# A two-layer transformer block on one core: attention's value products by four heads, row maxima over two banks, and first maxima made a row ahead

## The reference, cut to what matters

```
qkv = x @ w_qkv + b_qkv                      # (8, 512, 384), 16 heads of 8 channels
att = einsum('bhqd,bhkd->bhqk', q, k) / sqrt(8)
att = where(causal, att, -inf)
y   = einsum('bhqk,bhkd->bhqd', softmax(att), v)
x1  = x + gate * (y @ w_proj + b_proj)
```

## Time and profile before

| what | value |
|---|---|
| runs shown, median (lowest to highest) | 3398.66 us (3397.5 to 3406.68) |
| span of the profiled execution | 3389.5 us |
| outside the span, against the median | 9.2 us |
| PE busy / DVE / ACT / POOL | 76% / 55% / 47% / 28% |
| mean granted clock of TensorE | 0.834 |
| DMA, mean | 29 GB/s |

### The profile page before, as it was taken

The page is one execution under the profiler, slowest core; times in us unless marked ns, Lnnn a source line. Parts: engine busy times, 40 slices in busy tenths (PEclk is TensorE's granted clock), DMA queues, the critical chain, the costliest instruction groups (busy, mean ns, idle before and its releaser), DMA issues. The chain is left out here.

```text
span 3389.5 us, 65593 instructions
## 1 busy us (share of the span) xinstructions
PE 2579.8 (76%) x23476; PEld 1819.6 (54%) x23508; DVE 1865.9 (55%) x4776; ACT 1591.1 (47%) x3545; POOL 932.4 (28%) x641
## 2 busy tenths in 40 slices
PE   2486888778788787878879678786888868787787
PEld 1254764456644565446645367453664447644565
DVE  2337654576445664466643765537655476545664
ACT  0137453474435643365434754338443474435644
POOL 1105330143303432043220442105330143302332
PEclk8588887888878888788878888789887888878888
DMA  3300011010110101001020010200002000110101
GB/s 96 84 5 10 14 26 73 4 15 12 38 60 1 16 15 59 35 3 16 13 89 5 5 18 9 89 5 10 13 19 80 4 13 13 33 64 4 16 15 42
DMA packets 213726, 96.60 MB, mean 29 GB/s; under 512 B 175978, under 2 KB 204530, under 8 KB 209754
## 3 DMA queue, kind: packets, MB, share of 16 engines
q1 hardware_dynamic: 209160, 90.02, 10.0%
q10 hardware_dynamic: 4224, 2.10, 0.2%
HBM read 70.88 MB, written 21.17 MB: 27 GB/s over the span
## 5 line engine op out<-in xcount | busy, mean ns | idle before, releaser
L1695 POOL TENSOR_TENSOR arena<-upto,gk 128x1536 f32<-128x1536 f32 x32 | 88.1, 2754 | 941.2 <-DVE beta L1142 941.2
L1149 DVE SCALAR_TENSOR_TENSOR arena<-bank,conv,arena 128x510 f32<-128x510 f32 (+1 forms) x384 | 285.7, 748 | 71.4 <-ACT arena L1442 47.8
L1687 POOL TENSOR_TENSOR arena<-arena 128x511 f32<-128x511 f32 x192 | 243.9, 1270 | 205.1 <-DVE arena L1149 204.9
L1036 DVE TENSOR_REDUCE mx<-bank 128x1 f32<-128x128 f32 (+3 forms) x512 | 219.0, 486 | 136.2 <-PE bank L515 131.2
L678 PE MATMUL bank<-h_t,arena 128*128 128x512 f32 x384 | 228.3, 690 | 57.1 <-DVE arena L1149 57.0
L514 PE MATMUL bank<-vq 72*128 72x128 bf16 (+3 forms) x512 | 180.9, 414 | 98.3 <-DMA vq<-qk_bounce 49.7
L1405 ACT ACTIVATE arena<-bank 128x384 f32<-128x384 f32 (+1 forms) x384 | 174.1, 538 | 166.2 <-PE bank L542 166.2
L1527 ACT COPY u<-bank 32x192 f32<-32x192 f32 x128 | 39.9, 312 | 400.2 <-PE bank L812 398.7
L1739 POOL TENSOR_TENSOR arena<-arena 128x1536 f32<-128x1536 f32 x24 | 82.5, 3437 | 422.7 <-DVE arena L1278 227.3
L469 PE MATMUL bank<-ident,xn 128*128 128x128 f32 x132 | 36.8, 435 | 169.5 <-DVE xn L987 169.5
L735 PE MATMUL bank<-vq 64*128 64x128 f32 x1536 | 117.2, 305 | 57.5 <-ACT arena L1516 36.5
(11 more groups left out here) (290 smaller groups left out, 6435.6 us busy)
## 6 DMA issues: line engine op xcount, KB each, us to landing
arena<-w_bounce SPq DMA_DIRECT2D x16, 1024.0 KB, 8.5
vq<-qk_bounce SPq DMA_DIRECT2D x27, 384.0 KB
vq<-qk_bounce SPq DMA_DIRECT2D x9, 1152.0 KB
qk_bounce<-qkp SPq DMA_DIRECT2D x54, 128.0 KB, 2.3
arena<-in_L_attn_Wv_dram SPq DMA_DIRECT2D x8, 768.0 KB, 11.7
t<-t_bounce SPq DMA_DIRECT2D x256, 12.0 KB, 1.8
x<-t_bounce SPq DMA_DIRECT2D x256, 12.0 KB, 1.8
arena<-in_L_attn_Wq_dram SPq DMA_DIRECT2D x8, 384.0 KB, 8.7
```

The lines of the kernel that those rows point to most:

```text
L1036: last = V.reduce_max(mx[:, h, t:t + 1], score_bank(n)[:, 0:(t + 1) * P], AX.X)
L1149: ins = V.scalar_tensor_tensor(a[:, k:T], ps[:, 0:T - k], conv[:, n, 3 - k:4 - k], a[:, k:T], ALU.mult, ALU.add)
L1687: G.tensor_tensor(acc[:, n % 4, 1:T], acc[:, n % 4, 1:T], acc2[:, n % 3, 0:T - 1], ALU.add).then_inc(taps_added, 1)
```

## The change

It does these things.

- The maxima are made in 22 units of one instruction each: a unit is one query tile t of 8, 4, 2 or 2 heads, spread over two neighbouring banks (1024 or 768 columns), with one mask matmul per bank. All eight banks become one PSUM tensor, so that one reduction can span two.
- Heads are grouped by eight for the maxima: two groups, two trips through DRAM (`maxima(b, i)` on SP) in place of four.
- The first group of the next row (units 0 to 10, `scores(b, 1, u)` on PE and `row_max(b, 1, u)` on DVE) is made at the end of the row: units 0 and 1 between the transposes and the projection of `project(3)`, 2 and 3 before the last norm, 4 to 6 after the second, third and fourth feed-forward matmul, 7 to 10 after the second product; on DVE 7 to 10 and the splitting stand behind L1343. For the first row this is done ahead of the loop.
- The feed-forward matmuls use two banks in place of four and wait for the gelu of two before.
- Value products take four heads at once, with `p_t` in two buffers of four heads; each four heads are transposed (`turn`) and divided as soon as they are copied.
- `scores_t` has one mask matmul for the bank with two key tiles.
- The transfers into the stacks are twelve without broadcast, of 8 rows (nine for q) and 24 rows (three for k), in place of four; `stacks_in` goes from 80 to 208.
- POOL fills v's constant columns behind the splitting of q and k. SP serves the first maxima of a row before the loads of weights.

The diff, cut to its core (counts, bank tables and the parts that only follow are left out):

```diff
+        HALF = [(t, range(h, h + n)) for t, n in enumerate((8, 4, 2, 2)) for h in range(0, HG, n)]
+        NU = len(HALF)
+        UNITS = [(t, range(hs.start + HG * i, hs.stop + HG * i)) for i in range(2) for t, hs in HALF]
...
         def score_t_bank(h, i):
-            return PS[3 + i if h < 10 or h % 2 else i]
+            return PS[(3, 4, 6)[i] if h >= HG and h % 2 == 0 else i]
...
         def f_bank(j):
-            return PS[2 + j]
-
-        f2_bank = PS[6]
+            return PS[6 + j % 2]
+
+        f2_bank = PS[5]
...
             if c + 1 == NT:
-                stages += [("enter_qkv", 1), ("enter_q", 1), ("enter_k", 1)]
+                stages += [("enter_q", 1), ("enter_k", 1), ("enter_qkv", 1)]
...
+            def scores(b, ahead, u):
+
+                t, hs = UNITS[u]
+                if u == 0:
+                    pe.wait_ge(stacks_in, at(b, stacks_in, IN_ROW["stacks_in"], ahead))
+                    pe.wait_ge(v_ready, at(b, v_ready, 1, ahead))
+                elif u == NU:
+                    pe.wait_ge(s_max, at(b, s_max, NU - 1, ahead))
+                elif u != 1 and u != NU + 1:
+                    pe.wait_ge(s_max, at(b, s_max, u - 1, ahead))
+                e = (t + 1) * P
+                per_bank = len(hs) // 2
+                for i in range(2):
+                    ps = PS[unit_banks(u)[0] + i][:, 0:per_bank * e].rearrange("p (h w) -> p h w", h=per_bank)
+                    for j in range(per_bank):
+                        h = hs[per_bank * i + j]
+                        mm(ps[:, j, :], q_stack[0:KS, h, t * P:e], k_stack[0:KS, h, 0:e], start=(j == 0), stop=False)
+                    last = mm(ps[:, :, t * P:e], ident_bf[:, :], mask_q[:, 0:per_bank, :], start=False, stop=True)
+                last.then_inc(s_ps, 1)
...
+                def weigh(g):
+
+                    if g:
+                        pe.wait_ge(y_sb, at(b, y_sb, g))
+                    else:
+                        pe.wait_ge(v_pads, at(b, v_pads, 1))
+                        pe.wait_ge(x_done, at(b, x_done, 1))
+                    pe.wait_ge(p_ready, at(b, p_ready, 12 * g + 12))
                     c0 = 0
                     for j in range(NT):
                         n = T - j * P
-                        for h in (2 * pair, 2 * pair + 1):
-                            r = 32 * (h % 4)
-                            last = mm(y_bank[r:r + 32, j * P:T], v32[:, j, h, :], p_t[:, h % 4, c0:c0 + n],
+                        for i in range(4):
+                            last = mm(y_bank[32 * i:32 * i + 32, j * P:T], v32[:, j, 4 * g + i, :], p_t[g % 2][:, i, c0:c0 + n],
...
+                scores(b, 0, NU)
+                scores(b, 0, NU + 1)
+                move_maxima(0)
+                for u in range(NU + 2, NU + 6):
+                    scores(b, 0, u)
+                scores_t(0)
+                scores(b, 0, NU + 6)
+                scores_t(1)
+                scores(b, 0, NU + 7)
+                scores_t(2)
+                scores(b, 0, NU + 8)
+                scores(b, 0, NU + 9)
+                scores_t(3)
+                scores(b, 0, NU + 10)
+                scores_t(4)
+                weigh(0)
+                move_maxima(1)
+                for h in range(5, 9):
                     scores_t(h)
+                weigh(1)
+                scores_t(9)
+                turn(0)
+                for h in range(10, 13):
+                    scores_t(h)
+                weigh(2)
+                turn(1)
+                for h in range(13, HA):
+                    scores_t(h)
+                turn(2)
+                weigh(3)
+                turn(3)
...
+                    if c + 1 == NT:
+                        scores(b, 1, 0)
+                        scores(b, 1, 1)
+                    ps = wo_bank(c)
...
+                scores(b, 1, 2)
+                scores(b, 1, 3)
                 layer_norm(LEAVE)
...
                 for j in range(FT):
+                    if j >= 2:
+                        pe.wait_ge(f_sb, at(b, f_sb, j - 1))
                     mm(f_bank(j)[:, :], w1[:, j * P:(j + 1) * P], h_t[:, :], start=True, stop=True).then_inc(f_ps, 1)
+                    if j:
+                        scores(b, 1, 3 + j)
...
                 last.then_inc(f2_ps, 1)
-                pe.wait_ge(rt_d, at(b, rt_d, 1))
+                for u in range(7, NU):
+                    scores(b, 1, u)
...
+            def row_max(b, ahead, u):
+
+                t, hs = UNITS[u]
+                dve.wait_ge(s_ps, at(b, s_ps, u + 1, ahead))
+                dst = mx[:, hs.start:hs.stop, t].rearrange("p (i h) -> p i h", i=2)
+                V.reduce_max(dst, unit_scores(u), AX.X).then_inc(s_max, 1)
...
                 V.tensor_tensor(xs[:, :, :], xs[:, :, :], xn[:, :, :], ALU.add).then_inc(x_done, 1)
+                for u in range(7, NU):
+                    row_max(b, 1, u)
+                split_maxima(b, 1, 0)
...
                 for part in range(PARTS):
-                    of_part = qk_bounce[0, part].rearrange("d h t -> d (h t)").unsqueeze(0).to_broadcast([PARTS, DA, HA * T])
-                    sp.dma_start(q_stack[PARTS * DA * part:PARTS * DA * (part + 1), :, :].rearrange("p h t -> p (h t)"), of_part).then_inc(stacks_in, 16)
+                    of_part = qk_bounce[0, part].rearrange("d h t -> d (h t)")
+                    for r in range(PARTS * DA * part, PARTS * DA * (part + 1), DA):
+                        sp.dma_start(q_stack[r:r + DA, :, :].rearrange("p h t -> p (h t)"), of_part).then_inc(stacks_in, 16)
                 sp.wait_ge(parts_out[1], at(b, parts_out[1], 16 * PARTS, ahead))
-                all_parts = qk_bounce[1].rearrange("n d h t -> (n d) (h t)").unsqueeze(0).to_broadcast([PARTS, PARTS * DA, HA * T])
-                sp.dma_start(k_stack[0:KS, :, :].rearrange("p h t -> p (h t)"), all_parts).then_inc(stacks_in, 16)
+                all_parts = qk_bounce[1].rearrange("n d h t -> (n d) (h t)")
+                for r in range(0, KS, PARTS * DA):
+                    sp.dma_start(k_stack[r:r + PARTS * DA, :, :].rearrange("p h t -> p (h t)"), all_parts).then_inc(stacks_in, 16)
```

More of the change, by code:

```diff
@@ L85, in dram @@
             return nc.dram_tensor(name, shape, dt).ap()
-        PS = [ctx.enter_context(nc.psum_tensor(f"bank{i}", [P, 512], F32)) for i in range(8)]
+        banks = ctx.enter_context(nc.psum_tensor("bank", [P, 8 * 512], F32))
+        PS = [banks[:, 512 * i:512 * (i + 1)] for i in range(8)]
         def sig(name):
@@ L483, in enter_qkv @@
                 last.then_inc(v_ps, 1)
+            def scores(b, ahead, u):
[8 more added lines that the diff above has]
+                e = (t + 1) * P
+                per_bank = len(hs) // 2
+                for i in range(2):
[5 more added lines that the diff above has]
+                last.then_inc(s_ps, 1)
             enter_norm(0, 0)
             enter_qkv(0, 0)
+            for u in range(NU):
+                scores(0, 0, u)
             with pe.Fori(0, NB) as b:
@@ L559, in weigh @@
                     last.then_inc(pv_ps, 1)
-                LAG = 8
-                for h in range(LAG):
-                    scores(h)
-                    if h == 5:
-                        move_maxima(0)
-                for h in range(HA):
-                    if h + LAG < HA:
-                        scores(h + LAG)
-                    scores_t(h)
-                    if h in (1, 5, 9):
-                        move_maxima(h // 4 + 1)
-                    if h % 2 and h > 1:
-                        weigh(h // 2 - 1)
@@ L1028, in tiles @@
                     return ps[:, :].rearrange("p (c d) -> p c d", c=NT)
+                for u in range(NU, 2 * NU):
+                    row_max(b, 0, u)
+                split_maxima(b, 0, 1)
                 for g in range(4):
-                    for h in range(HG * g, HG * g + HG):
-                        for t in range(NT):
-                            n = h * NT + t
-                            dve.wait_ge(s_ps, at(b, s_ps, n + 1))
-                            last = V.reduce_max(mx[:, h, t:t + 1], score_bank(n)[:, 0:(t + 1) * P], AX.X)
-                            last.then_inc(s_max, 1)
@@ L1337, in _ @@
                 dve.wait_ge(dve_step, step())
+                for u in range(4, 7):
+                    row_max(b, 1, u)
                 dve.wait_ge(f2_ps, at(b, f2_ps, 1))
@@ L1797, in _ @@
             with sp.Fori(0, NB) as b:
+                maxima(b, 0)
                 sp.wait_ge(x_done, at(b, x_done, 1))
@@ L1806, in _ @@
                 sp.dma_start(wconv[:, 2 * nq:2 * nq + nv], L1_attn_Wv).then_inc(wc_in, 16)
[L1807 to L1811 removed]
+                maxima(b, 1)
                 tokens(b, 1)
```

192 lines of the change are left out of this document (92 added, 100 removed).

## The result

Four runs of the changed kernel have the median 3479.09 us (3476.32 to 3483.02); the kernel before, beside them, 3402.67. The ratio is 1.0229, 95% interval 1.0203 to 1.0255: slower by 76 us, where the forecast was 104 us faster. It came out near rival C, the stacks that come late. The first view is the page of the changed kernel: its span, and the second row of its costliest groups (busy us, mean ns, idle time of the engine just before, and what ended it).

The account below looks back on a forecast made before the run. Attention was taken as bound by TensorE and VectorE taking turns at low clock, then TensorE alone. Sum: -28.4 + 8 x 3 - 7 x 14.6 + 2.6 = -104.0, median 3294.7 us; forecast range 3255 to 3335 (0.60), wider range 3230 to 3365.

Parts of the forecast that it names:

- rival C: End of row: stacks land late, at 527.6, shifting zero (feed-forward end) by some 26 us, about 3500 us; chance 0.06.
- (9): End of row: stack copies on eight queues take 9.8 us and land at 507.6; output projection starts 4.0 us late.
- (12): First row: stacks land at 105.5, attention ends at 169.7 against 198.2; 28.4 us gained once.
- (1): Attention, VectorE: half the maxima move out; a unit of 1024 columns costs 1.14 us; DVE saves about 3 us per row.
- (2): After zero, the feed-forward part's end: first half's maxima stand at zero + 5.5; DVE's next reduction after the jump at 8.1.
- (3): Attention, TensorE at 1.2 GHz: restart at zero + 4.65, first value product at 26.0, where it stood at 30.3.
- (4): Attention: first maxima's bounce through DRAM is ready at 11 to 12, before the first transposed scores (13.4), so free.
- (5): Value products: four heads side by side take 2.3 us (3.9 at low clock); 4 x 2.3 us of TensorE less per row.
- Rival E: Value products: four heads take 4.6 us, as two pairs; 8.3 us per row, 3361 us; chance 0.10.
- (6): Attention: first product from zero + 26.0 to 29.6; after the second maxima's bounce, second half's heads may start at 34.0.
- (7): Later attention: ScalarE is the bound, 6.9 us per four heads; last product ends at zero + 51.0, copy 51.7.
- (8): Attention's tail: last transposes, normalisation and projection take 4.1 us, not 6.3; attention ends at 55.8 against 70.4.

Follow-up runs that it names:

- groups B, A and C: Copies of 16 KB rows timed without the computation: B the old four broadcasts (30.4 us), A the change's form (27.2 us), C copies of 24 rows (14.5 us).
- fast_copies: Changed kernel with stack rows reordered, so queries are one copy of 24 rows by 3 and keys three of 24 rows; 3384.1 us, ratio 0.9975.
- halves_pairs: fast_copies_halves with the value products of four heads issued as two pairs, one after the other; 3389.2 us, ratio 0.9971.
- fast_copies_halves: fast_copies with the first eight heads' half of every row copied first under its own semaphore; 3322.7 us, ratio 0.9794 to the kernel before.
- late_units: Changed kernel with the first eleven units of scores and maxima back at the top of the row; 3375.2 us, ratio 0.9925.

## Why the prediction was wrong, step by step

**(9) is the step that failed.** It read the share of 0.19 as the count of busy queues, which was right (0.60 now, and 0.19, 0.63 and 0.72 in groups B, A and C). It then took it that every queue brings 27 GB/s wherever it writes, which was wrong: "on eight queues the busiest has nine + six + one descriptors of 16 KB at 0.61 us". The 0.61 us is that of three queues. With eight and twelve queues on neighbouring partitions a packet took 1.9. By the forecast the stacks land 12.6 us after their issue (its own terms, 3.2 and 9.8, give 13.0); it was 29.3. The row that I had beside it, a share of 1.02 at 418 GB/s, was a load over 128 partitions, and I carried its rate over to rows on 8 partitions. In place of 3 us a row the rest lost 20.5, eight times, 140 us more than forecast: that alone turns -104 into +36; attention (+35) and the first row (+17) bring it to the 89 us of the spans.

By the Trainium skill (DMA: Bandwidth & Descriptors, Why a DMA increments its semaphore by 16 and not by 1) the copies have 3, 8 and 12 queues; the shares agree, and the rule says nothing of what a queue then moves.

Rival C had the mechanism and the size: 26 us a row and some 3500 us, against 20.5 and 3479. I gave it 0.06, although the only row that showed this very transfer showed 81 GB/s. Its point of decision, a shift of 16 a row, was too high, since it rested on the forecast's gains: with the measured ones it is (11.3 + 66.9 - 3.1)/8 = 9.4. fast_copies has 9.0 us more in the rest than the kernel before and a first row 22 us shorter, and is 0.25% faster; the changed kernel has 20.5 and is slower.

**The first row (12)** was forecast at 28.4 us earlier. It gained 11.3, for the same reason. With the fast halves it is 171.3 against 198.2, 26.9 us.

**Attention (1) to (8)** was to give 14.6 us a row and gave 9.6. The steps in order, in the changed kernel's third row (zero is 967.4), VectorE first:

```profile
970.96 1.23 DVE L1071 TENSOR_REDUCE mx<-bank 128x2 f32<-128x1024 f32 x1 [0.21 <-PE bank L521]
...
975.86 0.17 DVE L1093 COPY mod_b<-mod_t 128x8 f32 x1 [2.79 <-issue]
978.08 2.36 DVE L1071 TENSOR_REDUCE mx<-bank 128x8 f32<-128x1024 f32 x2 [2.05 <-issue]
```

```profile
973.63 0.60 PE L520 MATMUL bank<-vq 72*128 72x128 bf16 x4 [2.70 <-issue]
979.36 0.61 PE L520 MATMUL bank<-vq 72*128 72x256 bf16 x2 [2.46 <-DVE mx L1071]
982.15 0.50 PE L520 MATMUL bank<-vq 72*128 72x384 bf16 x1 [0.47 <-DVE mx L1071]
```

- (1) A unit of 1024 columns costs 1.18 us (two in 2.36) where 1.14 was forecast, and (2) the first half's maxima stand at zero + 5.7 where it was 5.5: right.
- (3) TensorE restarts at zero + 6.3, not 4.65, and VectorE's first reduction after the jump comes at 10.7, not 8.1. I had counted one jump and no start behind it; VectorE has two gaps, 2.79 and 2.05. TensorE waits for it, and the first product starts at 29.2 in place of 26.0. That is 3.2 of the 5 us. The granted clock stays at 0.50 that much longer too, to zero + 32, where 29 was forecast.
- (4) The bounce of the first maxima is free; that of the second half makes TensorE wait about 1 us a row.
- (5) Four heads in 3.89 us when begun at the low clock and 2.36 at the high one, for 3.9 and 2.3: right. Rival E, forecast at 8.3 us a row, is priced at 7.5 by halves_pairs, since two pairs take 3.9 us, not 4.6; the 3.96 of the earlier trace rows had shown that. By the Trainium skill (TensorE: Matmul & The Clock Gate, Measured speedup vs the span model) about 2.7 us was the estimate, and the measured 2.36 decides: four column groups lose next to nothing here.
- (6), (7) The working of (6) has the first product 3.6 us long where (5) has 3.9; its 34.0 follows with 3.9. The last product ends at zero + 55.2 in this row, where 51.0 was forecast; after the 3.2 us there is 1 more here. In four of the seven rows the granted clock fell to 0.5 once more, 38 us after zero and for 3.4 us, and those rows have attention at 61.0 to 62.0 where the others have 59.5 to 60.0.
- (8) From the last product's end to L1121 4.7 us, forecast 4.8: right. (10), (11) With the wait gone the rest is 1.7 us longer (fast_copies_halves); forecast 3: right, and the units beside the feed-forward part cost at most that (late_units, without them, has a rest of 339.1 for its 338.8). (13) 3.1 us, forecast 2.6. The 9.2 us that the forecast carried as lying outside the span were 1.7 in the changed kernel's profiled run.

With the stacks on time, the forecast's sum can be held against a kernel in which its assumption holds: fast_copies_halves has a span of 3316.8, forecast 3285.5. The 31 us are attention, 5.5 x 7 = 39 too short, less 1.3 x 8 = 10 in the rest, and 2 in the first row and the tail together.

## What to carry to other kernels

A share of busy queues is not a rate. Before a copy is given more queues, look at which partitions they write at one time, and take its duration from a row with the same destination, not from a load over 128 partitions. When work is moved ahead in an engine's order, everything queued behind its first wait moves with it: ask for the landing time of what it reads first, and split the transfer so that this part comes first. And a rival that rests on the one row which shows the disputed transfer itself deserves more than 0.06.

## What the runs showed of the hardware

- Nine copies of 8 rows of 16 KB took 17.0 us to neighbouring partitions and 7.6 us to every ninth one, with the queues nearly equally busy (0.49 and 0.46): 1.9 us a packet against 0.8.
- Three queues alone moved 77 GB/s, eight to neighbours 69, twelve on 24 rows 164, sixteen over all partitions 308 to 328.
- Reading the same 8 rows of DRAM for 128 partitions cost 10.0 us against 6.8 from 128 rows.
- Four fp32 value products on 32 columns each ran side by side in 2.36 us, where two such pairs in a row took 3.89.
